# Pre-activation convolution of sign images: thresholds moved to GpSimd, the first conv half's eviction moved ahead of the signs, and three edits of the start

## The reference

```python
B = sign(W - mean + us[m] * std)              # 5 binary filters, us = -1 .. 1
alpha = solve(Bf.T @ Bf, Bf.T @ wf)           # 5 coefficients
W_eff = einsum('m,mhwio->hwio', alpha, B)     # 3x3x32x32
X = groupnorm(x)                              # per image and channel
out = 0
for n in range(3):
    A = sign(clip(X + v[n], 0, 1) - 0.5)
    out = out + beta[n] * (conv(A, W_eff) + sum(alpha) * bias[n])
return x + out
```

## Time and profile before

| | |
|---|---|
| median of 3 runs | 206.68 us (206.48 to 207.05) |
| the profiled execution | 206.35 us |
| its span in the profile | 204.6 us |
| busy share of the span | PE 82%, DVE 84%, ACT 68%, POOL 31% |
| mean granted TensorE clock | 0.995 of full speed |
| moved by DMA | 39.61 MB, mean 194 GB/s |

### The profile page before, as it was taken

The page is one execution under the profiler, slowest core; times in us unless marked ns, Lnnn a source line. Parts: engine busy times, 40 slices in busy tenths (PEclk is TensorE's granted clock), DMA queues, the critical chain, the costliest instruction groups (busy, mean ns, idle before and its releaser), DMA issues.

```text
span 204.6 us, 4766 instructions
## 1 busy us (share of the span) xinstructions
PE 167.0 (82%) x1800; PEld 128.9 (63%) x1800; DVE 171.6 (84%) x422; ACT 139.9 (68%) x183; POOL 62.7 (31%) x76
## 2 busy tenths in 40 slices
PE   1596166489898989898989898989899999789871
PEld 0484065266767676767676767777777776658560
DVE  5449999998999999999999999999999999875241
ACT  2626557287888878787878787878787878673110
POOL 6174243543333333232323232414141414240000
PEclk9999999999999999999999999999999999999998
DMA  4799333061688979797889787978797464657625
GB/s 113 228 268 272 94 81 85 0 163 51 193 233 240 265 215 262 212 256 221 239 240 262 216 254 226 255 224 253 227 251 229 131 187 137 181 149 211 194 67 157
DMA packets 21030, 39.61 MB, mean 194 GB/s; under 512 B 9744, under 2 KB 9744, under 8 KB 21008
## 3 DMA queue, kind: packets, MB, share of 16 engines
q1 hardware_dynamic: 20272, 39.27, 67.9%
q10 hardware_dynamic: 736, 0.04, 0.2%
HBM read 13.15 MB, written 12.85 MB: 127 GB/s over the span
## 4 chain that ended last, share of the span: by engine, by line
PE 49%; ACT 19%; DVE 16%; issue 7%; DMA 6%; SPq 2%; ACTq 0%; DVEq 0%
PE conv_ps L723 24%; PE y_ps L743 13%; ACT signs L348 13%; PE x_ps L685 9%; ACT y_ch L361 6%; DMA x_nat<-in_x 4%; DMA s_odd<-s_even 3%; DVE raw_stats L555 2%; DVE y_nat L546 2%; DVE twice_dev L582 1%; DVE s_even L612 1%; DVE s_even L617 1%; PE x_ps L693 1%; DVE neg_thr L591 1%; PE conv_ps L782 1%
## 5 line engine op out<-in xcount | busy, mean ns | idle before, releaser
L723 PE MATMUL conv_ps<-s_even,w_mm 128*64 128x448 f16 (+1 forms) x576 | 102.9, 332 | 3.0 <-DVE w_mm L518 1.6
L726 PE MATMUL conv_ps<-s_odd,w_mm 128*64 128x448 f16 (+2 forms) x576 | 102.9, 320 | 0.0
L348 ACT ACTIVATE signs<-x_ch,neg_thr 128x784 f16<-128x784 f32 x96 | 85.0, 940 | 2.2 <-DVE neg_thr L591 2.2
L723 PEld LDWEIGHTS conv_ps<-s_even,w_mm 128*64 128x64 f16 x576 | 60.5, 110 | 30.4 <-issue 5.0
L726 PEld LDWEIGHTS conv_ps<-s_odd,w_mm 128*64 128x64 f16 x576 | 60.6, 110 | 0.0
L546 DVE SCALAR_TENSOR_TENSOR y_nat<-y_ps,y_const,x_nat 112x1024 f32<-112x1024 f32 (+1 forms) x32 | 36.6, 1145 | 10.2 <-PE y_ps L743 10.2
L306 POOL TENSOR_SCALAR lo_part<-signs,ratio_lo 128x1568 f16<-128x1568 f16 x16 | 25.5, 1595 | 62.3 <-ACT signs L348 62.2
L685 PE MATMUL x_ps<-ident,x_nat 112*128 112x112 f32 x224 | 31.8, 290 | 13.4 <-ACT x_ch L343 10.1
L743 PE MATMUL y_ps<-ident,y_ch 128*112 128x128 f32 x224 | 31.2, 279 | 11.3 <-ACT y_ch L361 9.9
L310 POOL TENSOR_SCALAR lo_part<-signs,ratio_lo 128x1568 f16<-128x1568 f16 x16 | 26.6, 1664 | 44.9 <-DVE half_hi L605 44.9
L343 ACT ACTIVATE x_ch<-x_ps 128x896 f32<-128x896 f32 (+1 forms) x32 | 26.1, 815 | 19.5 <-PE x_ps L685 19.5
(11 more groups left out here) (106 smaller groups left out, 92.5 us busy)
## 6 DMA issues: line engine op xcount, KB each, us to landing
x_nat<-in_x SPq DMA_DIRECT2D x16, 448.0 KB, 5.1
out<-y_nat SPq DMA_DIRECT2D x16, 448.0 KB, 3.8
s_odd<-s_even SPq DMA_DIRECT2D x32, 203.0 KB, 2.8
s_odd<-s_even SPq DMA_DIRECT2D x32, 188.5 KB, 3.0
x_nat<-in_x SPq DMA_DIRECT2D x16, 336.0 KB, 4.7
out<-y_nat SPq DMA_DIRECT2D x16, 322.0 KB, 2.6
s_odd<-s_even SPq DMA_DIRECT2D x32, 14.5 KB, 2.7
x_nat<-in_x SPq DMA_DIRECT2D x16, 14.0 KB, 5.3
```

The lines of the kernel that those rows point to most:

```text
L348: act.activation(signs[q % 2][:, n, :, a, :], x_ch[q % CH_SLOTS][:, :, a, :], ACT.Sign, bias=neg_thr[q % 2][:, n, a:a + 1]).then_inc(signe ...
L723: last = nc.tensor.matmul(low[:, 0:n * ROWS], wt, s_even[b][:, part, r0:r0 + 2 * n, t:t + H], start=first, stop=end)
L726: last = nc.tensor.matmul(high[:, 0:m * ROWS], wt, s_odd[b][:, part, r0:r0 + 2 * m, t:t + H], start=first, stop=end and not at_edge)
```

## The change

1. The thresholds of a pair, other than the reciprocal, go from DVE to POOL: there they are five operations, each linked to the one ahead by a semaphore, behind the two `lo_part` of the pair before.
2. `scale_out(p+1, 0)` stands ahead of `copy_in(p+4, 1)` and `begin_signs(p+3)` in ACT's turn. Only in turn -1 does `begin_signs(2)` stay ahead of it. In the start `begin_signs(0)` goes ahead of `copy_in(1, 1)`.
3. The sum over the five filters is one product into `w_parts` (960 elements per partition) and one `reduce_sum`, in place of five instructions.
4. The parameters land on one partition and are spread by a matmul and one copy by DVE out of PSUM.
5. `gather_lanes(0)` is ahead of `bring_in(1, 0)` on PE, and `bring_in(1, 0)` now waits for the moments of pair 0.
6. In POOL's start, `order_beta` and `split_ratios` come behind the two memsets of `filt`'s corners; on DVE the reciprocal for the ratios comes behind `eliminate(1)`.

```diff
@@ gpsimd
+            def thresholds(q):
+                mom = moments[q % 2]
+                pool.wait_ge(moments_ready, 2 * (q + 1))
+                link(ts(twice_dev[:, 0, :], mom[:, :, 1], GN_EPS, 1.0, ALU.add, ALU.mult))
+                pool.wait_ge(inv_ready, q + 1)
+                link(tt(twice_dev[:, 1, :], twice_dev[:, 0, :], inv_root[:], ALU.mult))
+                link(tt(twice_dev[:, 2, :], twice_dev[:, 1, :], root[:], ALU.add))
+                link(tt(scaled_dev[:], twice_dev[:, 2:3, :].broadcast_to([128, N_ACT, 2]),
+                        order[:, 1, :].unsqueeze(2).broadcast_to([128, N_ACT, 2]), ALU.mult))
+                tt(neg_thr[q % 2][:], scaled_dev[:], mom[:, :, 0].unsqueeze(1).broadcast_to([128, N_ACT, 2]),
+                   ALU.subtract).then_inc(thr_ready, 1)
...
             pool.wait_ge(corners_zero, 2)
-            weigh_low(0)
-            pool.wait_ge(lo_weighed, 2)
+            order_beta()
+            thresholds(0)
+            split_ratios()
+            pool.wait_ge(ratios_ready, 3)
+            pool.wait_ge(thr_ready, 1)
+            weigh_low_first(0)
+            weigh_low_second(0)
+            thresholds(1)
+            pool.wait_ge(thr_ready, 2)
...
             for q in range(1, PAIRS):
-                weigh_low(q)
+                weigh_low_first(q)
+                weigh_low_second(q)
+                if real(q + 1):
+                    thresholds(q + 1)
@@ scalar
-            act.dma_start(params[:, 1, :], v.partition_broadcast(128)).then_inc(params_loaded, 16)
-            act.dma_start(params[:, 0, :], beta.partition_broadcast(128)).then_inc(params_loaded, 16)
-            act.dma_start(params[:, 2, :], bias.partition_broadcast(128)).then_inc(bias_loaded, 16)
+            for i, t in enumerate((beta, v, bias)):
+                act.dma_start(params_row[:, i, :], t.unsqueeze(0)).then_inc(params_loaded, 16)
...
                 if real(p + LEAD):
                     copy_in(p + LEAD, 0)
-                    copy_in(p + LEAD, 1)
-                if real(p + 3):
-                    begin_signs(p + 3)
                 if p == -1:
+                    begin_signs(2)
                     act.wait_ge(y_scale_ready, 1)
                 if real(p + 1):
                     scale_out(p + 1, 0)
+                if real(p + LEAD):
+                    copy_in(p + LEAD, 1)
+                if real(p + 3) and p != -1:
+                    begin_signs(p + 3)
...
             copy_in(1, 0)
+            begin_signs(0)
             copy_in(1, 1)
-            begin_signs(0)
@@ vector
-                link(ts(neg_w, fl[0], neg_alpha[:, 0:1], None, ALU.mult))
+                link(tt(w_parts[:], fl, neg_alpha.unsqueeze(1).broadcast_to([128, TAPS * 2 * C, M_FIL]), ALU.mult))
                 mark(nc.vector.reduce_sum(size[:, 0:1], w_stat[:, 6:11], axis=AX.X))
-                link(stt(neg_w, fl[1], neg_alpha[:, 1:2], neg_w, ALU.mult, ALU.add))
...
+                link(nc.vector.reduce_sum(neg_w, w_parts[:], axis=AX.X))
...
             def invert_root(q):
                 dve.wait_ge(root_ready, q + 1)
-                return mark(nc.vector.reciprocal(inv_root[:], root[:]))
+                if q:
+                    dve.wait_ge(thr_ready, q)
+                nc.vector.reciprocal(inv_root[:], root[:]).then_inc(inv_ready, 1)
...
-                    make_thresholds(r, add_root(divide_variance(r, invert_root(r))))
+                    invert_root(r)
...
+            dve.wait_ge(params_spread, 1)
+            nc.vector.tensor_copy(params[:].rearrange("p i n -> p (i n)"), params_ps).then_inc(params_ready, 1)
...
-            dve.wait_ge(divisor_ready, 1)
-            nc.vector.reciprocal(tmp[:, 5, 2:3], tmp[:, 5, 1:2]).then_inc(inverse_ready, 1)
-            dve.wait_ge(order_ready, 3)
-            thresholds(0)
+            invert_root(0)
...
             eliminate(1)
+            dve.wait_ge(divisor_ready, 1)
+            nc.vector.reciprocal(tmp[:, 5, 2:3], tmp[:, 5, 1:2]).then_inc(inverse_ready, 1)
@@ tensor
+            pe.wait_ge(params_loaded, 48)
+            nc.tensor.matmul(params_ps, ones[0:1, :], params_row[:].rearrange("p i n -> p (i n)"),
+                             start=True, stop=True).then_inc(params_spread, 1)
             pe.wait_ge(ident_ready, 1)
...
-            bring_in(1, 0)
             gather_lanes(0)
...
+            pe.wait_ge(moments_ready, 2)
+            bring_in(1, 0)
             bring_in(1, 1)
```

More of the change, by code:

```diff
@@ L67, in preact_conv_kernel @@
         inv_root = sb("inv_root", [128, 2])
-        twice_dev = sb("twice_dev", [128, 2])
+        twice_dev = sb("twice_dev", [128, 3, 2])
+        scaled_dev = sb("scaled_dev", [128, N_ACT, 2])
         neg_thr = [sb(f"neg_thr{i}", [128, N_ACT, 2]) for i in range(2)]
@@ L77, in preact_conv_kernel @@
         eps_col = sb("eps_col", [128, 1])
+        params_row = sb("params_row", [1, 3, N_ACT])
         params = sb("params", [128, 3, N_ACT])
@@ L100, in preact_conv_kernel @@
         size = sb("size", [128, 3])
+        w_parts = sb("w_parts", [128, TAPS * 2 * C, M_FIL])
         w_eff = sb("w_eff", [128, TAPS, 2, C])
@@ L111, in preact_conv_kernel @@
         w_sum_ps = conv_ps[0][:, 0, 0:2]
+        params_ps = conv_ps[1][:, 0, 0:3 * N_ACT]
         gram_ps = conv_ps[0][0:GP, 0, 0:GP]
@@ L124, in preact_conv_kernel @@
         root_ready = sem("root_ready")
+        inv_ready = sem("inv_ready")
         thr_ready = sem("thr_ready")
@@ L144, in preact_conv_kernel @@
         params_loaded = sem("params_loaded")
-        bias_loaded = sem("bias_loaded")
+        params_spread = sem("params_spread")
+        params_ready = sem("params_ready")
         w_loaded = sem("w_loaded")
@@ L297, in _, with weigh_low_first @@
             pool.tensor_copy(filt[0:96, :, 0, :, M_FIL], w_raw[0:96, :, 0, :]).then_inc(w_copied, 1)
-            order_beta()
-            split_ratios()
-            pool.wait_ge(ratios_ready, 3)
-            def weigh_low(q):
+            def thresholds(q):
[9 more added lines that the diff above has]
+                   ALU.subtract).then_inc(thr_ready, 1)
+            def weigh_low_first(q):
                 pool.wait_ge(signed, 6 * q + 2)
@@ L364, in begin_signs @@
             def begin_signs(q):
-                act.wait_ge(thr_ready, 3 * (q + 1))
+                act.wait_ge(thr_ready, q + 1)
                 if real(q - 2):
@@ L502, in filter_parts @@
                 neg_w = w_eff[:].rearrange("p a o c -> p (a o c)")
-                fl = [filt[:, :, :, :, m].rearrange("p a o c -> p (a o c)") for m in range(M_FIL)]
+                fl = filt[:].rearrange("p a o c m -> p (a o c) m")[:, :, 0:M_FIL]
                 dve.wait_ge(corners_zero, 2)
                 mark(stt(w_stat[:, 6:11], neg_alpha, -1.0, neg_alpha, ALU.mult, ALU.max))
-                link(ts(neg_w, fl[0], neg_alpha[:, 0:1], None, ALU.mult))
+                link(tt(w_parts[:], fl, neg_alpha.unsqueeze(1).broadcast_to([128, TAPS * 2 * C, M_FIL]), ALU.mult))
                 mark(nc.vector.reduce_sum(size[:, 0:1], w_stat[:, 6:11], axis=AX.X))
-                link(stt(neg_w, fl[1], neg_alpha[:, 1:2], neg_w, ALU.mult, ALU.add))
-                mark(nc.vector.reciprocal(size[:, 1:2], size[:, 0:1]))
+                link(nc.vector.reduce_sum(neg_w, w_parts[:], axis=AX.X))
+                link(nc.vector.reciprocal(size[:, 1:2], size[:, 0:1]))
+                link(ts(size[:, 2:3], size[:, 1:2], -W_SCALE, None, ALU.mult))
                 dve.wait_ge(order_ready, 3)
@@ L512, in filter_parts @@
                     .then_inc(y_scale_ready, 1)
-                link(stt(neg_w, fl[2], neg_alpha[:, 2:3], neg_w, ALU.mult, ALU.add))
-                mark(ts(size[:, 2:3], size[:, 1:2], -W_SCALE, None, ALU.mult))
-                link(stt(neg_w, fl[3], neg_alpha[:, 3:4], neg_w, ALU.mult, ALU.add))
-                link(stt(neg_w, fl[4], neg_alpha[:, 4:5], neg_w, ALU.mult, ALU.add))
                 wm = [w_mm[:, i].rearrange("p a o c -> p (a o c)") for i in range(3)]
@@ L576, in invert_root @@
                 dve.wait_ge(root_ready, q + 1)
-                return mark(nc.vector.reciprocal(inv_root[:], root[:]))
-            def divide_variance(q, n):
-                dve.wait_ge(moments_ready, 2 * (q + 1))
-                settle(n)
-                return mark(stt(twice_dev[:], moments[q % 2][:, :, 1], GN_EPS, inv_root[:], ALU.add, ALU.mult))
-            def add_root(n):
-                settle(n)
-                return mark(tt(twice_dev[:], twice_dev[:], root[:], ALU.add))
-            def make_thresholds(q, n):
-                settle(n)
-                for m in range(N_ACT):
-                    stt(neg_thr[q % 2][:, m, :], twice_dev[:], order[:, 1, m:m + 1], moments[q % 2][:, :, 0],
-                        ALU.mult, ALU.subtract).then_inc(thr_ready, 1)
-            def thresholds(q):
-                make_thresholds(q, add_root(divide_variance(q, invert_root(q))))
+                if q:
+                    dve.wait_ge(thr_ready, q)
```

(1 more changed line is left out.)

5 lines of the change are left out of this document (2 added, 3 removed).

## The result

| | before | after |
|---|---|---|
| median, measured beside each other | 206.58 us (4 runs, 205.46 to 207.05) | 213.8 us (4 runs, 213.34 to 214.27) |
| ratio after / before | | 1.036, 95% interval 1.031 to 1.041 |
| span of the profiled execution | 204.6 us | 212.2 us |
| mean granted TensorE clock | 0.995 | 0.989 |

The account below looks back on a forecast made before the run. PE was taken as the bound, with 9.71 us of work and 0.63 idle per 10.34 us turn. 206.35 + 1.25 (start) - 1.9 (turns) - 0.2 (tail) = 205.5 us, 205.8 as a median; 8-in-10 range 199.0 to 207.4.

Parts of the forecast that it names:

- The eviction order: ACT's turn: `y_ch` done by 113.8, 3 us before PE wants it; worth PE's whole 0.63 us wait per turn.
- The collision of the chain with `sum_low`: POOL's last threshold operation, at E + 1.01, comes 0.08 us after `sum_low` starts on DVE and stands until E + 1.90.
- E: Time mark in each turn: the end of DVE's sum at L612, `sum_high` at L619 in the changed kernel.
- The turn: Mid-kernel loop with the block: 10.18 us against 10.34, so 12 turns give back 1.9 us.
- The first turn: DVE reaches E at 4.66, PE allows `y_nat` at 4.62; DVE later by 0.04 us, so `sum_low` blocks the chain.
- a free turn holds itself: In an unblocked turn `sum_low` is PE-bound, some 0.25 us behind the last POOL operation, so the state persists.
- Rival 1: The threshold chain slips through ahead of `sum_low`: turn 9.71 us, time 199.5 us as a median; chance 0.3.
- Rivals 2 and 4: 2: first POOL operation takes ports ahead of L612, turn 10.41, 208.9 us; 4: turn stays 10.34, 207.7 us; chance 0.12 together.
- Start-up: Before the loop: E of the first turn at 52.1 against 50.84, costing 1.25 us.
- rival 3: Parameters land late, over 3.4 us after issue, delaying the start; at 5.5 us, 2.1 us more: 207.9 us; chance 0.08.
- Tail: Last pairs: later `signs` offset by `y_ch` no longer between them, `sum_low` of pair 14 earlier; gain 0.2 us.

Follow-up runs that it names:

- experiment 1: Kernel before with only the eviction of the first conv half moved ahead of the second copy and the signs: 203.06 us, ratio 0.975; run again, 0.986.
- experiment 5: Kernel before plus one small unused POOL operation per pair ahead of the second `lo_part`, with two SBUF inputs in even pairs, one in odd: 206.86 us against 207.39.
- experiment 13: Changed kernel with one tiny DVE instruction between `y_nat` and `sum_low`: 204.73 us, ratio 0.989.
- experiment 3: Changed kernel with the thresholds back on DVE, all else as changed: 205.75 us, ratio 0.989.
- experiment 8: Kernel of experiment 3 with the five-instruction sum over the filters again: 203.55 us, ratio 0.979.
- experiment 9: Kernel of experiment 3 with the three spread parameter DMAs again, without matmul and copy: 204.29 us, ratio 0.986.
- experiment 12: Kernel of experiment 3 with both filter sum and parameter DMAs as before: 204.43 us, ratio 0.985.
- experiment 10: Changed kernel with two `bn_stats` of pair p+4 moved between `y_nat` and `sum_low`, from turn 0 on: 208.9 us, ratio 1.009.
- experiment 14: Changed kernel with three tiny DVE instructions between `y_nat` and `sum_low`: 205.13 us, ratio 0.985.
- experiment 6: Changed kernel with the threshold chain as six POOL operations of one tensor input each, other values as one-column scalars: 227.69 us, ratio 1.097.

## Why the prediction was wrong

Against the profiled execution the forecast was 205.5 us and the result 214.09, 8.6 more. Nearly all of it is in three terms: 6.0 in the turns (-1.9 forecast, +4.09 measured), 1.7 in the start (+1.25 and +2.97) and 0.8 in the tail (-0.2 and +0.6). The step that failed first of all is the one that says when GpSimd begins to be held.

- **The eviction order:** right. It gives back PE's wait (experiment 1, 2.5% and 1.4%), up to DVE's sum, 9.94 us; I had read 10.03 from the earlier trace rows.
- **The collision of the chain with `sum_low`:** the pair of instructions was named, and it does decide the case. My step was "the last POOL operation would come 0.08 too late, and stand until E + 1.90". It failed there: I let an operation be held only if it starts after `sum_low` has started. In fact the first dependent one is held, from E + 0.22, 0.69 us before the sum starts, while `y_nat` is under way with the sum next behind it and free of waits. Three more links of 0.28 and a hop then follow the end of the sum instead of running ahead of it: `signs` at E + 2.79 instead of E + 2.02, 0.77 us late in each turn. The Trainium skill (SBUF — State Buffer, Who interferes with whom) says that the order of issue decides which engine blocks. I had read "issue" as "start". The traces agree on the pair of instructions and on the wait to the sum's end, and they fit the page's word if a sum counts as issued once its own waits are over, even while the instruction ahead of it still runs: so it was 42 times out of 42, and where the sum still had to wait, POOL was not held (experiment 5). That this is what happens inside the engine no run shows.
- **The turn:** 10.67, not 10.18. It closes as E to `signs` 2.79; four `signs` in a row until the second `hi_part` can start, 3.50 (110.02 to 113.52); from there to the next E 4.39 (113.52 to 117.91). The sum is 10.68. My path, through `lo_part` and `spread_stats`, had 8.16 behind the start of `signs`, this one has 7.89. So the hold adds 0.77 and the rest is 0.27 shorter: 0.50, the difference between 10.18 and 10.67 within rounding.
- **The first turn:** I had DVE later than PE by 0.04, "so the block strikes". In turn 0 it was the other way round: PE held `y_nat` back by 1.25 us and the chain was free. DVE passed that wait on: its turn was 9.40 of its own plus 1.25, 10.65. In turn 1 PE held `y_nat` back by only 0.23 us, and the second dependent operation, 0.19 us into it, stood for 1.76; from turn 2 on `y_nat` followed the reciprocal at once, and the first one is held. My argument that a free turn holds itself fails in the changed kernel and holds in experiment 13, where the tiny instruction takes the block away.
- **Rival 1, the free turn of 9.71:** the number was right and its condition wrong. It needs the shield, and then it is 9.67. Its time, 199.5, left out the start's real cost and that the shift transfers are the next bound.
- **Rivals 2 and 4:** L619 took 1.25 us as before, so the first POOL operation didn't get ahead of it. The engines together do not need 10.34 us either: experiments 1 and 13 have 9.94 and 9.67. No case of mine had a turn above 10.41; the range ended at 207.4 since all my slow cases priced one lock, of one instruction.
- **Start-up, forecast +1.25, measured +2.97.** "(0.247 - 0.15)/96 = 1.0 ns per element for the product" was the wrong end of my own bounds: the product took 1.91 us ((1.91 - 0.15)/960 = 1.83 ns), the sum 1.14, together 3.05 where I took 2.6. "I take 2.7" for the parameters: the last row landed 4.26 us after issue and PE began `bring_in(0,0)` at 6.89, not 5.67; rival 3, cheaper than its example, was true besides. Over all traces the transposes begin at 5.67 to 6.88 with the old parameter DMAs (nine traces, middle one 5.95) and at 6.31 to 7.56 with the new ones (nine, middle one 6.70), so some 0.75 of these 1.22 us are the change. And a POOL operation was held in the start too, behind the product, which reads two SBUF tensors. Instructions in order of time:

```profile
6.37 0.59 PE L781 MATMUL conv_ps<-params_row,ones 1*128 1x9 f32 x2 [1.76 <-DMA params_row<-in_L_conv_bias]
...
6.89 1.75 PE L693 MATMUL x_ps<-ident,x_nat 112*128 112x112 f32 x8
...
30.01 1.91 DVE L534 TENSOR_TENSOR w_parts<-filt,neg_row 128x960 f32<-128x960 f32 x1
30.16 1.84 POOL L310 TENSOR_TENSOR twice_dev<-twice_dev,inv_root 128x2 f32<-128x2 f32 x1
...
32.03 1.14 DVE L536 TENSOR_REDUCE w_eff<-w_parts 128x192 f32<-128x960 f32 x1
```

  By experiments 3, 8, 9 and 12 the 2.97 are 0.96 for the thresholds on POOL, 1.84 for filter sum and parameters together, and 0.17 for the rest. Only the 1.00 of the filter sum is clear of the spread of 0.84 us between two profiles of one kernel; the other shares, and the 2.97 itself, are known no better than that (the six traces with the changed start have their first `y_nat` at 50.50 to 51.48).
- **Tail, forecast -0.2, measured +0.6.** The turn that holds the last thresholds (0.98) is blocked like the others; behind it 0.38 came back.
- **What is shown and what is argued.** Shown: that POOL is held under `y_nat` when `sum_low` is next and not when another instruction is (experiments 5, 10, 13, 14), and that the operations with one tensor input are held like those with two (6). Argued only: that the lock is taken by the queued sum itself, and that its waits must be over; no kernel was made in which only that wait changes. Open: whether DVE would hold POOL under instructions other than `y_nat` with a two-input one behind them.

## What to carry to other kernels

Before moving a chain of small dependent operations to GpSimd, list where in VectorE's queue the two-SBUF-input instructions stand, and count the instruction ahead of each as locked too, unless the two-input one still waits for a semaphore then: a chain in which one link is caught pays the lock and then all its later links. If such a move is wanted, a tiny one-input instruction ahead of the two-input one costs 0.07 us and here took a microsecond off the turn. And when an instruction is moved later to make room, look first which transfer it feeds.
